# A Mamba, cross-attention and mixture-of-experts decoder layer on one core: the norm shift and seven FFN products move from VectorE to GpSimd, and all five orders are written anew

## The chip, the cores and the metric

One core of a Trainium2 chip runs the whole layer in one program. The metric is device time in microseconds (us) of that program; lower is better. The engines are called by their names in the profile: PE (TensorE), with its weight loads as PEld, DVE (VectorE), ACT (ScalarE), POOL (GpSimd) and SP (SyncE, which issues the DMAs here).

## What is computed

128 sequences of 64 tokens with 128 features, all in float32, go through three blocks. Each block adds its result to its input and normalises the sum over the features.

```python
x = layernorm(x + mamba(x))          # RMS norm, in-projection, 4-tap conv, silu, selective scan with 16 states, gate, out-projection
x = layernorm(x + xattn(x, ctx))     # 16 heads of width 8, over the 64 tokens of the same sequence's context
x = layernorm(x + moe(x))

def moe(xf):                         # 8 routed experts of width 176, top 2, and a shared one
    scores = softmax(xf @ w_router.T)
    topk_w, topk_idx = top_k(scores, 2)
    topk_w = topk_w / (topk_w.sum(-1) + 1e-20)
    cw = (one_hot(topk_idx, 8) * topk_w[..., None]).sum(1)
    eo = einsum(silu(xf @ wg) * (xf @ wu), wd)
    return einsum('te,teh->th', cw, eo) + silu(xf @ wg_s) * (xf @ wu_s) @ wd_s

def layernorm(x): return (x - mean(x)) / sqrt(var(x) + 1e-5)
```

## The kernel before

The tokens are cut into 16 chunks of 8 sequences, 512 tokens each. A full tile is 128 partitions by 512 columns. A chunk goes through these steps, under the names that the order lists use:

- `squares`, `mean`, `scaled`, `xnT`, `hid`, `gate`, `tap`, `taps`, `tanh`, `silu`, `gated_h`, `xp`, `less`, `dt`, `soft`, `soft_ln`, `delta`: the part of the Mamba block ahead of its scan.
- `decay`, `B_row`, `drive`, `scan`, `prod`, `y_sum`: the scan. For each of the 16 states and each of two halves of 128 channels ACT makes a decay tile, DVE a scan (L881), POOL the product with C (L1011) and PE adds that up in PSUM (L503). The scan tiles are 512 columns wide, before and after. For the four states in `JOINED`, POOL first adds two products (L1015), so PE has fewer sums.
- `gated`, `mout`, `stats`, `shift`, `norm`, `x1T`: out-projection and first LayerNorm. The three LayerNorms are numbered by halves: stats0 and stats1 the first, stats2 and stats3 the second, stats4 and stats5 the third.
- `k`, `v`, `q`, and `km` or POOL's `k`: the keys, eight times over with all but one head pair masked out (the tile `km`; POOL makes five of the eight masked copies, L1047 and L1050, ACT three). Then for each of 8 sequences `score` (PE), the row maximum (DVE, L932), `exp` (ACT, L767, eight pieces), `sum` (DVE, the reciprocal `rden`, L936), `scale` (POOL, L1056), `turn` (PE transposes, L575), `mix` (PE, L583), then `aout`.
- second LayerNorm, `x2T`, `route` (PE, L596), the router's arithmetic `route`, `r_rank`, `r_cw` on DVE and POOL, and `cwT`, which goes to DRAM (`cw_out`) and comes back spread over partitions (`cw_in`, slots `cwr`, two of them).
- the FFN: 13 tiles of 128 hidden features. PE makes `up_g` and `up_u` of a tile (L599), ACT the tanh of g (L806), DVE `(tanh + 1) * g` into `ga` (L979) and `ga * u` into `acts[i]` (L984), and POOL multiplies the first 11 tiles by the routing weights (`cw`, L1069). `down` (PE, L609 and L615) sums them up. The third LayerNorm and `out` end the chunk.

Two buffers tie the steps of neighbouring chunks together. `acts[0..7]` lie in the same memory as `km`, so the masked keys of a chunk can be written only after `down` of the chunk before it has read them, and that FFN's tiles only after the attention of its own chunk. `ga` lies in `kT`. The eight PSUM banks are two for `p_drive`, two for the sums `p_y` and a ring of four (`p_ring`) that all other PE results share, in the order in which PE makes them.

A norm's `stats` step makes mean and variance on DVE (L852, L856), POOL adds eps (L1028) and raises to the power -0.5 (L1031), DVE makes the shift `-mean * rstd` (L926), and ACT applies both (L791).

Each engine runs a fixed list of steps, once per turn: `ORDER_TEXT` gives it and it is written out in the file. A word such as `back.up_g3` means: step up_g3 of the chunk that is one turn behind the scan. `head`, `front`, `scan`, `back` and `tail` are chunks +2, +1, 0, -1 and -2 against the turn's own. So the list of a turn holds steps of up to five chunks side by side. An engine waits at a step until its inputs are there, and whatever stands behind it in the list waits too; the waits are semaphores.

## Time and profile before

| what | value |
|---|---|
| median of 3 runs | 2048.26 us (2046.75 to 2048.63) |
| the profiled execution's own time | 2052.23 us |
| its span, first to last instruction | 2050.4 us |
| mean granted PE clock | 0.934 of full speed |
| PE busy | 1716.5 us, 84% |
| DVE busy | 1687.0 us, 82% |
| ACT busy | 1362.9 us, 66% |
| POOL busy | 1418.6 us, 69% |
| DMA queue of SP | 23.9% of 16 engines |

No engine is full, and the lists are the same in each turn, so a middle turn can be read as one period. In a timeline each row has its start in us from the span's start, the duration of the group in us, the engine, the source line, the operation, the tiles written and read, and in brackets how long the engine sat idle before it and what ended the wait. Successive instructions overlap by some 0.1 us in the records, so the step from one start to the next is a little less than a duration.

### The profile page before, as it was taken

To read this page: it belongs to the slowest core of one execution; us is meant where nothing else is said; L and a number is where in the kernel's file an instruction comes from. 1 tells how busy PE (TensorE), PEld (TensorE's weight loads), DVE (VectorE), ACT (ScalarE), POOL (GpSimd) and SP (SyncE) were. 2 spreads that over 40 slices of the span, in tenths; PEclk is the share of its full clock that TensorE was granted. 3 is DMA by queue.
4 is the path that set the end of the run, shared out by engine and by line. 5 is a ranking of instruction groups with operands and counts; after the bars stand their busy time and mean duration, and the time that the engine had idled before them with its cause. 6 is when DMAs were issued, how large, how long until landed. Compare 5 with 4: busy or idle time off the path is not lost. (4 is left out here: it accounts for less than half of the span.)

```text
span 2050.4 us, 26488 instructions
## 1 busy us (share of the span) xinstructions
PE 1716.5 (84%) x7047; PEld 1002.7 (49%) x7138; DVE 1687.0 (82%) x2369; ACT 1362.9 (66%) x4258; POOL 1418.6 (69%) x1300
## 2 busy tenths in 40 slices
PE   3668897989889898988988898898989889897967
PEld 1224464545446454544645454464545546454544
DVE  3798888989888897988889898888988889887623
ACT  3569577685957768495775848677594866757361
POOL 0587677867767686777768687776867777686733
PEclk8779999999999999999999999999999999998988
DMA  3212322213232122323212232221222222122202
...
DMA packets 125926, 140.56 MB, mean 69 GB/s; under 512 B 44049, under 2 KB 69457, under 8 KB 125777
## 3 DMA queue, kind: packets, MB, share of 16 engines
q1 hardware_dynamic: 125776, 138.86, 23.9%
...
## 5 line engine op out<-in xcount | busy, mean ns | idle before, releaser
L1011 POOL TENSOR_TENSOR prod<-state,c_rep 128x512 f32<-128x512 f32 x512 | 668.5, 1313 | 87.6 <-DVE state L881 80.2
L881 DVE TENSOR_TENSOR_SCAN state<-decay,p_drive 128x512 f32<-128x512 f32 x512 | 610.4, 1206 | 25.0 <-ACT decay L637 17.3
L503 PE MATMUL p_y<-prod,ident 128*128 128x512 f32 x768 | 410.3, 621 | 6.0 <-POOL prod L1011 2.8
L637 ACT ACTIVATE decay<-delta,a_neg 128x504 f32<-128x504 f32 x512 | 364.7, 719 | 63.9 <-DVE state L881 60.5
L868 DVE TENSOR_TENSOR p_drive<-u,p_drive 128x1024 f32<-128x1024 f32 x256 | 312.3, 1220 | 69.6 <-PE p_drive L485 64.5
L767 ACT ACTIVATE ex<-p_ring,nmax 128x64 f32<-128x64 f32 x1024 | 305.5, 338 | 11.2 <-DVE nmax L932 9.5
L599 PE MATMUL p_ring<-x2T,wg 128*128 128x512 f32 x416 | 232.3, 643 | 6.5 <-DVE kT L979 6.5
L767 ACT ACTIVATION_READ_ACCUMULATOR ex<-p_ring,nmax 128x1 f32 x1024 | 237.4, 232 | 0.0
L1056 POOL TENSOR_TENSOR ex<-ex,rden 128x512 f32<-128x512 f32 x128 | 133.4, 1042 | 139.8 <-DVE rden L936 111.3
L806 ACT ACTIVATE gt<-p_ring 128x512 f32<-128x512 f32 x208 | 122.7, 590 | 160.1 <-PE p_ring L599 160.1
L599 PE MATMUL p_ring<-x2T,wu 128*128 128x512 f32 x416 | 217.4, 612 | 10.8 <-DVE kT L979 10.1
L503 PEld LDWEIGHTS p_y<-prod,ident 128*128 128x128 f32 x768 | 145.7, 199 | 142.4 <-issue 117.0
L1069 POOL TENSOR_TENSOR km<-km,cwr 128x512 f32<-128x512 f32 x128 | 162.6, 1271 | 26.9 <-DMA cwr<-cw_rows 26.6
L1015 POOL TENSOR_TENSOR prod<-prod 128x512 f32<-128x512 f32 x128 | 163.8, 1280 | 10.0
L583 PE MATMUL p_ring<-exT,vm 128*128 128x128 f32 x1024 | 143.4, 284 | 23.7 <-ACT exT L776 23.0
L583 PEld LDWEIGHTS p_ring<-exT,vm 128*128 128x128 f32 x1024 | 129.9, 194 | 65.8 <-issue 43.6
L979 DVE SCALAR_TENSOR_TENSOR kT<-gt,p_ring 128x512 f32<-128x512 f32 x208 | 140.4, 675 | 16.6 <-ACT gt L806 12.0
L570 PE MATMUL p_ring<-km,qs 128*128 128x512 f32 x256 | 132.0, 608 | 21.8 <-POOL km L1050 17.0
L575 PE MATMUL p_ring<-ident,ex 128*128 128x128 f32 x512 | 83.0, 287 | 78.9 <-POOL ex L1056 73.7
L599 PEld LDWEIGHTS p_ring<-x2T,wu 128*128 128x128 f32 x416 | 79.8, 198 | 115.0 <-issue 78.2
L615 PE MATMUL p_ring<-wd,km 128*128 128x128 f32 x1024 | 126.6, 277 | 4.7 <-POOL acts_more L1069 4.7
L791 ACT ACTIVATE x<-p_ring,shift,rstd 128x128 f32<-128x128 f32 x192 | 77.6, 461 | 73.9 <-DVE shift L926 73.9
...
## 6 DMA issues: line engine op xcount, KB each, us to landing
c_rep<-c_rows SPq DMA_DIRECT2D x256, 256.0 KB, 3.9
...
```

What stands on the lines that cost most here:

```text
L503: pe.matmul(p_y[1 - first][:], ident[:], prod[:, k % BUFFERS, :], start=False, stop=n == STATE - 1).then_inc(prod_used.sem, 1)
L583: mm = pe.matmul(p[:, 0:128], vm[:, i, q, :], exT[:, q, :], start=q == 0, stop=q == QUADS - 1)
L599: mm = pe.matmul(p[:], (wg if name == "up_g" else wu)[:, i, :], x2T[:], start=True, stop=True)
L637: act.activation(decay[:, j, :].rearrange("p (b t) -> p b t", t=SEQ)[:, :, 1:], delta[:, c.parity, j, :].rearrange("p (b t) -> p b t", t=S ...
L767: e = act.activation(ex[:, i % 2, a, :], p[:, a * SEQ:(a + 1) * SEQ], ACT.Exp, bias=nmax[:, i % 2, a:a + 1], accum_out=den[:, i % 2, a:a + 1])
L868: dve.tensor_tensor(p_drive[:], u[:, c.parity, :, :], p_b.unsqueeze(1).to_broadcast([128, HALVES, T]), ALU.mult).then_inc(drive_ready.sem, 1)
L881: dve.tensor_tensor_scan(state[:, k % BUFFERS, :], decay[:, j, :], p_drive[:, j, :], 0.0, ALU.mult, ALU.add).then_inc(state_ready.sem, 1)
L979: dve.scalar_tensor_tensor(ga, gt[:, i % 2, :], 1.0, p[:], ALU.add, ALU.mult).then_inc(free(name, i), 1)
L1011: pool.tensor_tensor(prod[:, k % BUFFERS, :], state[:, k % BUFFERS, :], c_rep[:, n % C_SLOTS, :], ALU.mult).then_inc(prod_ready.sem, 1)
L1015: pool.tensor_tensor(prod[:, k % BUFFERS, :], prod[:, k % BUFFERS, :], prod[:, (k - HALVES) % BUFFERS, :], ALU.add).then_inc(join_ready.se ...
L1056: pool.tensor_tensor(ex[:, i % 2, :, :], ex[:, i % 2, :, :], by_group(rden[:, i % 2, :]).to_broadcast([128, PAIRS, SEQ]), ALU.mult).then_i ...
L1069: pool.tensor_tensor(acts[i], acts[i], cwr[:, slot, :], ALU.mult).then_inc(act_ready.sem, 1)
```

## The change

`ON_POOL` names seven of the 13 FFN tiles. For these DVE writes `(tanh + 1) * g` straight into `acts[i]`, ACT copies u out of PSUM into one of two new tiles `us`, and a new POOL step `gu` multiplies the two; `cw` of that tile waits for it. The other six tiles are as before. ACT's copy of the third and later of the seven waits until POOL has used the same `us` tile, two tiles back.

The shift of all six norm halves is made by POOL: `nmean = -mean` beside the variance, then `shift = nmean * rstd` after `rstd`. DVE's `shift` step is gone.

The router's 1e-20 is a ninth column of `r_sel`, filled once, so that the sum over nine columns has it in, and the separate addition (L966) is gone. A reserve of memory for software DMAs is cut to 1024 bytes, which makes room for `us`; no DMA of this kernel is issued that way.

The order lists are new for all five engines, and are cut at another place of the period. Two lines of POOL's list stand for them in the diff.

```diff
--- before.py
+++ after.py
@@ -64,6 +64,7 @@
 ROUTED = EXPERTS * EXPERT_I // 128
+ON_POOL = (1, 2, 4, 5, 7, 8, 10)
 ROW_B, ROW_C = RANK, RANK + 3 * STATE
@@ -73,70 +74,68 @@
...
-        "scan.prod9 scan.prod10 scan.prod11 scan.prod12 back.scale3 scan.prod13 scan.prod14 "
...
+        "tail.cw10 back.stats0 back.stats1 scan.prod2 tail.stats4 scan.prod3 back.k0 tail.stats5 "
+        "scan.prod4 scan.prod5 back.scale0 scan.prod6 scan.prod7 back.scale1 scan.prod8 scan.prod9 "
@@ -256,7 +255,7 @@
         mhalf = sb("mhalf", [128, GROUPS])
-        eps = sb("eps", [128, 3])
+        eps = sb("eps", [128, 5])
 
@@ -288,6 +287,7 @@
         var = sb("var", [128, 3, GROUPS])
+        nmean = sb("nmean", [128, 3, GROUPS])
         rstd = sb("rstd", [128, 3, GROUPS])
@@ -313,7 +313,7 @@
         r_rank = sb("r_rank", [128, GROUPS, EXPERTS])
-        r_sel = sb("r_sel", [128, GROUPS, EXPERTS])
+        r_sel = sb("r_sel", [128, GROUPS, EXPERTS + 1])
         r_cw = sb("r_cw", [128, GROUPS, 128])
@@ -321,6 +321,7 @@
         r_gt, r_eq = pairwise[:, 0], pairwise[:, 1]
+        us = sb("us", [128, 2, T])
         acts_more = sb("acts_more", [128, FFN_TILES - CHUNK_B, T])
@@ -375,8 +376,9 @@
             signal(n, CHUNK_B) for n in ("max_ready", "rden_ready", "scale_ready"))
-        route_v, route_exp, route_g = signal("route_v", 11), signal("route_exp"), signal("route_g", 2)
+        route_v, route_exp, route_g = signal("route_v", 10), signal("route_exp"), signal("route_g", 2)
         gt_ready, act_ready = signal("gt_ready", FFN_TILES), signal("act_ready", ROUTED)
+        u_copied, gu_ready = signal("u_copied", len(ON_POOL)), signal("gu_ready", len(ON_POOL))
 
@@ -599,7 +601,7 @@
                 elif name == "cwT":
-                    pe.wait_ge(route_v.sem, route_v.at(c.m, 10))
+                    pe.wait_ge(route_v.sem, route_v.at(c.m, 9))
                     for g in range(GROUPS):
@@ -804,6 +806,14 @@
                     act.activation(gt[:, i % 2, :], p[:], ACT.Tanh, scale=0.5).then_inc(gt_ready.sem, 1)
+                elif name == "up_u":
+                    k = ON_POOL.index(i)
+                    p = filled(act, name, i, c.m)
+                    if k >= 2:
+                        act.wait_ge(gu_ready.sem, gu_ready.at(c.m, k - 2))
+                    elif c.m >= 1:
+                        act.wait_ge(gu_ready.sem, gu_ready.at(c.m - 1, len(ON_POOL) - 2 + k))
+                    act.activation(us[:, k % 2, :], p[:], ACT.Copy).then_inc(free(name, i), 1)
                 elif name == "cwT":
@@ -824,6 +834,8 @@
             dve.memset(eps[:, 1:3], LN_EPS)
+            dve.memset(eps[:, 3:5], -1.0)
+            dve.memset(r_sel[:, :, EXPERTS:], TOP_EPS)
             dve.memset(r_cw[:], 0.0).then_inc(consts_v.sem, 1)
@@ -919,12 +931,6 @@
                     ln_statistics(c, ln, half, filled(dve, LN_IN[ln], half, c.m))
-                elif name == "shift":
-                    ln, half = divmod(i, 2)
-                    g = slice(2 * half, 2 * half + 2)
-                    dve.wait_ge(ln_rstd[ln].sem, ln_rstd[ln].at(c.m, half))
-                    dve.scalar_tensor_tensor(shift[:, ln, g], mv[:, ln, g, 0], -1.0, rstd[:, ln, g],
-                                             ALU.mult, ALU.mult).then_inc(ln_shift[ln].sem, 1)
                 elif name == "score":
@@ -958,25 +964,28 @@
                     dve.wait_ge(route_v.sem, route_v.at(c.m, 5))
-                    dve.scalar_tensor_tensor(r_sel[:], r_rank[:], float(TOP), r_prob[:], ALU.is_lt, ALU.mult
+                    dve.scalar_tensor_tensor(r_sel[:, :, 0:EXPERTS], r_rank[:], float(TOP), r_prob[:], ALU.is_lt, ALU.mult
                                              ).then_inc(route_v.sem, 1)
...
                     dve.wait_ge(route_v.sem, route_v.at(c.m, 7))
-                    dve.tensor_scalar(r_max[:], r_sum[:], TOP_EPS, None, ALU.add).then_inc(route_v.sem, 1)
+                    dve.reciprocal(r_rec[:], r_sum[:]).then_inc(route_v.sem, 1)
                     dve.wait_ge(route_v.sem, route_v.at(c.m, 8))
-                    dve.reciprocal(r_rec[:], r_max[:]).then_inc(route_v.sem, 1)
-                    dve.wait_ge(route_v.sem, route_v.at(c.m, 9))
                     if c.m >= 1:
                         emptied(dve, "cwT", 0, c.m - 1)
-                    dve.tensor_tensor(r_cw[:, :, 0:EXPERTS], r_sel[:], by_group(r_rec[:]).to_broadcast(wide), ALU.mult
+                    dve.tensor_tensor(r_cw[:, :, 0:EXPERTS], r_sel[:, :, 0:EXPERTS], by_group(r_rec[:]).to_broadcast(wide), ALU.mult
                                       ).then_inc(route_v.sem, 1)
...
                     dve.wait_ge(gt_ready.sem, gt_ready.at(c.m, i))
-                    if i > 0:
-                        emptied(dve, "up_u", i - 1, c.m)
-                    dve.scalar_tensor_tensor(ga, gt[:, i % 2, :], 1.0, p[:], ALU.add, ALU.mult
+                    if i in ON_POOL:
+                        to = acts[i]
+                    else:
+                        to = ga
+                        last = max((j for j in range(i) if j not in ON_POOL), default=None)
+                        if last is not None:
+                            emptied(dve, "up_u", last, c.m)
+                    dve.scalar_tensor_tensor(to, gt[:, i % 2, :], 1.0, p[:], ALU.add, ALU.mult
                                              ).then_inc(free(name, i), 1)
@@ -1025,11 +1034,15 @@
                     pool.wait_ge(ln_aggr[ln].sem, ln_aggr[ln].at(c.m, half))
-                    pool.tensor_tensor(var[:, ln, g], mv[:, ln, g, 1], eps[:, 1:3], ALU.add
+                    pool.tensor_tensor(var[:, ln, g], mv[:, ln, g, 1], eps[:, 1:3], ALU.add)
+                    pool.tensor_tensor(nmean[:, ln, g], mv[:, ln, g, 0], eps[:, 3:5], ALU.mult
                                        ).then_inc(ln_var[ln].sem, 1)
...
                                        ).then_inc(ln_rstd[ln].sem, 1)
+                    pool.wait_ge(ln_rstd[ln].sem, ln_rstd[ln].at(c.m, half))
+                    pool.tensor_tensor(shift[:, ln, g], nmean[:, ln, g], rstd[:, ln, g], ALU.mult
+                                       ).then_inc(ln_shift[ln].sem, 1)
                 elif name == "add_out_b":
@@ -1062,8 +1075,16 @@
                     pool.tensor_tensor(r_gt, r_gt, r_eq, ALU.add).then_inc(route_g.sem, 1)
+                elif name == "gu":
+                    emptied(pool, "up_g", i, c.m)
+                    emptied(pool, "up_u", i, c.m)
+                    pool.tensor_tensor(acts[i], acts[i], us[:, ON_POOL.index(i) % 2, :], ALU.mult
+                                       ).then_inc(gu_ready.sem, 1)
                 elif name == "cw":
-                    emptied(pool, "up_u", i, c.m)
+                    if i in ON_POOL:
+                        pool.wait_ge(gu_ready.sem, gu_ready.at(c.m, ON_POOL.index(i)))
+                    else:
+                        emptied(pool, "up_u", i, c.m)
                     slot = i % CW_SLOTS
@@ -1146,7 +1167,7 @@
     arrays = {k: np.ascontiguousarray(v) for k, v in arrays.items()}
-    nc = bacc.Bacc("TRN2", target_bir_lowering=False, num_devices=1)
+    nc = bacc.Bacc("TRN2", target_bir_lowering=False, num_devices=1, dynamic_dma_scratch_size=1024)
     args = {k: nc.dram_tensor(f"in_{k}", v.shape, mybir.dt.from_np(v.dtype), kind="ExternalInput").ap()
...
```

How the instructions stand now is shown at three places. First, POOL between the router's ranking (L1061 and L1064 before, L1074 and L1077 now, tile x1T) and the first FFN tiles. Before:

```order
L1061 TENSOR_TENSOR x1T<-x1T,tri 128x256
L1064 TENSOR_TENSOR x1T<-x1T 128x256
L1011 TENSOR_TENSOR prod<-state,c_rep 128x512
L1015 TENSOR_TENSOR prod<-prod 128x512
L1011 TENSOR_TENSOR prod<-state,c_rep 128x512
L1015 TENSOR_TENSOR prod<-prod 128x512
L1011 TENSOR_TENSOR prod<-state,c_rep 128x512
L1023 TENSOR_TENSOR rms<-ms,mhalf 128x4
L1011 TENSOR_TENSOR prod<-state,c_rep 128x512
L1069 TENSOR_TENSOR km<-km,cwr 128x512 x2
```

and in the changed kernel, where L1081 is the new step `gu` and L1090 is `cw`:

```order
L1077 TENSOR_TENSOR x1T<-x1T 128x256
L1020 TENSOR_TENSOR prod<-state,c_rep 128x512
L1024 TENSOR_TENSOR prod<-prod 128x512
L1081 TENSOR_TENSOR km<-km,us 128x512
L1020 TENSOR_TENSOR prod<-state,c_rep 128x512
L1024 TENSOR_TENSOR prod<-prod 128x512
L1020 TENSOR_TENSOR prod<-state,c_rep 128x512
L1090 TENSOR_TENSOR km<-km,cwr 128x512
L1081 TENSOR_TENSOR km<-km,us 128x512
L1090 TENSOR_TENSOR km<-km,cwr 128x512
L1081 TENSOR_TENSOR km<-km,us 128x512
L1090 TENSOR_TENSOR km<-km,cwr 128x512
```

Products of the scan have moved out of this stretch, and the new multiplications stand in their place.

Second, POOL around the masked keys (km), between two of the scan's joins. Before:

```order
L1015 TENSOR_TENSOR prod<-prod 128x512
L1039 TENSOR_TENSOR x1b<-x,rowb 128x512
L1028 TENSOR_TENSOR var<-mv,eps 128x2
L1031 TENSOR_TENSOR rstd<-var,mhalf 128x2
L1047 TENSOR_TENSOR km<-kT,masks 128x8x64
L1050 TENSOR_SCALAR km<-kT,masks 128x8x64 x4
```

and in the changed kernel:

```order
L1024 TENSOR_TENSOR prod<-prod 128x512
L1060 TENSOR_TENSOR km<-kT,masks 128x8x64
L1063 TENSOR_SCALAR km<-kT,masks 128x8x64 x4
L1037 TENSOR_TENSOR var<-mv,eps 128x2
L1038 TENSOR_TENSOR nmean<-mv,eps 128x2
L1041 TENSOR_TENSOR rstd<-var,mhalf 128x2
L1044 TENSOR_TENSOR shift<-nmean,rstd 128x2
```

The last half of the third norm, which stood ahead of the keys, stands behind them, and the sum into x1b has moved to a later place.

Third, DVE at the first sequences of the attention: nmax is the row maximum, rden the reciprocal of the sum, h and gate are full tiles of the Mamba part. Before:

```order
L932 TENSOR_REDUCE nmax<-p_ring 128x8
L899 SCALAR_TENSOR_TENSOR h<-h,zc 128x512 x2
L903 SCALAR_TENSOR_TENSOR gate<-gate,gh 128x512
L932 TENSOR_REDUCE nmax<-p_ring 128x8
L936 RECIPROCAL rden<-den 128x8
L881 SCALAR_TENSOR_TENSOR state<-decay,p_drive 128x512
```

and in the changed kernel:

```order
L938 TENSOR_REDUCE nmax<-p_ring 128x8
L893 SCALAR_TENSOR_TENSOR state<-decay,p_drive 128x512
L938 TENSOR_REDUCE nmax<-p_ring 128x8
L942 RECIPROCAL rden<-den 128x8
L911 SCALAR_TENSOR_TENSOR h<-h,zc 128x512
L938 TENSOR_REDUCE nmax<-p_ring 128x8
```

Ahead of the first rden there now stand a scan and the second row maximum, where the two h tiles, a gate tile and the second row maximum stood.

## Rows read from the trace of the kernel before

**Rows 1.** The page's head line.

```profile
span 2050.4 us, 26488 instructions
```

**Rows 2.** One DVE line of the router, once per chunk: duration, start in us.

```profile
L956 DVE TENSOR_TENSOR x1T<-r_prob x1: 418/418/418, 215.8 to 215.8; 128x256 f32<-128x256 f32 x1
...
L956 DVE TENSOR_TENSOR x1T<-r_prob x1: 419/419/419, 1780.0 to 1780.0; 128x256 f32<-128x256 f32 x1
```

**Rows 3.** Busy us (x instructions) of PE, PEld, DVE, ACT, POOL; clock, DMA.

```profile
1055.45:1099.03 43.58, 42.21 (x115) 19.29 (x117) 38.56 (x56) 22.39 (x48) 33.60 (x28) 0.94 0.37 110
1099.03:1113.76 14.73, 14.68 (x122) 13.84 (x122) 12.75 (x27) 6.53 (x14) 10.94 (x14) 1.00 0.01 2
1113.76:1119.21 5.45, 4.09 (x21) 2.56 (x21) 5.42 (x7) 5.39 (x15) 5.45 (x7) 1.00 0.00 0
1119.21:1166.82 47.61, 39.50 (x172) 23.00 (x175) 40.85 (x51) 43.07 (x183) 36.74 (x32) 1.00 0.29 78
1166.82:1174.96 8.14, 3.77 (x17) 2.62 (x16) 6.62 (x9) 7.24 (x11) 2.46 (x4) 0.71 0.00 0
sum 119.51, PE 104.25 PEld 61.31 DVE 104.19 ACT 84.62 POOL 89.20; mean PE 20.85 PEld 12.26 DVE 20.84 ACT 16.92 POOL 17.84
```

**Rows 4.** Timeline around down's end and the masked keys.

```profile
1111.75 0.38 PE L551 MATMUL p_ring<-ident,x 128*128 128x128 f32 x2
...
1111.97 1.02 PE L494 MATMUL p_y<-h,diag_d 128*128 128x512 f32 x2
...
1113.76 1.04 POOL L1047 TENSOR_TENSOR km<-kT,masks 128x512 f32<-128x512 f32 x1
```

**Rows 5.** Timeline at the attention's first sequence.

```profile
1120.95 2.80 DVE L899 SCALAR_TENSOR_TENSOR h<-h,zc 128x512 f32<-128x512 f32 x2
...
1123.19 0.34 ACT L767 ACTIVATE ex<-p_ring,nmax 128x64 f32<-128x64 f32 x1
...
1123.68 1.75 DVE L903 SCALAR_TENSOR_TENSOR gate<-gate,gh 128x512 f32<-128x512 f32 x1
...
1125.95 0.19 DVE L936 RECIPROCAL rden<-den 128x8 f32<-128x8 f32 x1
...
1127.47 0.63 PE L575 MATMUL p_ring<-ident,ex 128*128 128x128 f32 x4 [3.51 <-POOL ex L1056]
```

**Rows 6.** Timeline from the second norm's last half to the FFN.

```profile
1167.88 0.20 POOL L1028 TENSOR_TENSOR var<-mv,eps 128x2 f32<-128x2 f32 x1 [0.74 <-DVE mv L856]
1168.16 0.71 POOL L1031 TENSOR_TENSOR rstd<-var,mhalf 128x2 f32<-128x2 f32 x1
...
1168.90 1.22 DVE L926 SCALAR_TENSOR_TENSOR shift<-mv,rstd 128x2 f32<-128x2 f32 x1
...
1171.10 0.79 ACT L791 ACTIVATE x<-p_ring,shift,rstd 128x128 f32<-128x128 f32 x2
...
1173.26 1.85 PE L596 MATMUL p_ring<-wrt,x2T 128*128 128x8 f32 x8 [0.56 <-ACT x2T L796]
```

**Rows 7.** First and last routing product of the period on POOL.

```profile
1072.05 1.27 POOL L1069 TENSOR_TENSOR km<-km,cwr 128x512 f32<-128x512 f32 x1 [0.46 <-DMA cwr<-cw_rows]
...
1099.56 1.26 POOL L1069 TENSOR_TENSOR acts_more<-acts_more,cwr 128x512 f32<-128x512 f32 x1
```

**Rows 8.** Groups by line and shape: busy us, mean ns | idle before, releasers.

```profile
L881 DVE TENSOR_TENSOR_SCAN state<-decay,p_drive 128x512 f32<-128x512 f32 x512 | 610.4, 1206 | 25.0 <-ACT decay L637 17.3 <-POOL prod L1011 0.7
...
L984 DVE TENSOR_TENSOR km<-kT,p_ring 128x512 f32<-128x512 f32 x128 | 87.9, 686 | 36.6 <-PE p_ring L599 27.9 <-DVE kT L979 0.5
...
L776 ACT ACTIVATE exT<-p_ring 128x512 f32<-128x512 f32 x128 | 77.5, 606 | 15.8 <-PE p_ring L575 12.9 <-PE p_ring L583 0.6
...
L966 DVE TENSOR_SCALAR r_max<-r_sum 128x4 f32<-128x4 f32 x16 | 15.4, 965 | 0.6
```

**Rows 9.** Lines of their own: ns min/median/max, first and last start.

```profile
L926 DVE SCALAR_TENSOR_TENSOR shift<-mv,rstd x96: 146/994/1236, 147.2 to 2046.1; 128x2 f32<-128x2 f32 x96
...
L899 DVE SCALAR_TENSOR_TENSOR h<-h,zc x32: 666/1200/1754, 32.7 to 1724.1; 128x512 f32<-128x512 f32 x32
```

115 rows, old and new, of the table ORDER_TEXT are left out of this document.

## The prediction, made before the changed kernel ran

> **What bounds the kernel now.** I read the head line first [rows 1], then one router line that runs once per chunk: from its first start to that of chunk 13 there are 13 equal periods in 1564.2 us, 120.3 us each [rows 2]. The kernel is these periods, with 215.8 us ahead and 270 us behind in which fewer stages run. The view by stretches of one such period (119.5 us) shows what kind of bound it is [rows 3]: in the sum PE is busy 104.3 us, DVE 104.2, POOL 89.2, ACT 84.6. No engine is the limit over the period; each is the limit somewhere. What closes into a ring is one chunk's way through the shared memory of `km` and `acts`: masked keys, attention, second norm, router, FFN, down, and then the next chunk's keys. Its length is the period, so I price the change along that ring, in the five stretches of [rows 3]: FFN up to the start of down 43.6 us, down to the start of the keys 14.7, keys 5.5, attention 47.6, and from its end to the first FFN product 8.1. What each is short of can be read there: the FFN stretch has PE at 42.2 and DVE at 38.6 of 43.6; attention has ACT at 43.1 of 47.6; the last has everything waiting, and the PE clock falls to 0.71.
>
> **Work moved, per chunk.** DVE loses seven products of 0.69 us (4.8) [rows 8], six shifts (median 0.99, least 0.15, so 4 to 6, [rows 9]) and one addition of 0.97 [rows 8]: about 10 of 104 us. ACT gains seven copies out of PSUM, by the nearest row (a 128x512 copy, 0.61) 4.3 us [rows 8]: 88.9. POOL gains seven products of 1.27 [rows 7] and twelve two-column operations, by the variance row 0.20 each [rows 6], 11.3 in all: 100.5 of 119.5. POOL goes from third to first or second.
>
> **Down to the keys.** POOL starts the masked keys at 1113.76, though down's last product was through by 1111.75 when PE took the next step; between them stands the third norm's half [rows 4]. In the new list that half stands behind the keys: 1.9 us less, if the join ahead of them ends in time. Two pairs of x1T transposes now stand between the halves of down, 0.22 us each by the distance of the starts in [rows 4]: 0.45 more. Sum -1.45; from -1.9 to -0.5 if POOL is late by one product. Keys to first score: 0, PE waits for them now as before.
>
> **Attention.** In its first sequence the last exp piece ends at 1123.5, but its reciprocal is at 1125.95, because two h tiles and a gate tile stand ahead of it on DVE; the first transposes wait for POOL's scale until 1127.47, 3.51 us of idle PE [rows 5]. The new DVE list has the reciprocal right behind the second row maximum: 2.4 us less. On ACT one pair of dt copies leaves the stretch, 1.2 us by [rows 8], and ACT is what is full here. Against that POOL gets 4.2 us more work between keys and last scale: two bias additions (2.5), one norm half (1.3) and 0.4 for the other. POOL idles 10.9 us in the stretch now [rows 3], and every scale has to come in time. So the bounds are -3.6 (POOL's new work fits its gaps) and +0.6 (all of it is on the path). I find no row that settles it and take the middle, -1.5.
>
> **Second norm to FFN.** Now: POOL's rstd ends at 1168.87, DVE's shift takes 1.22 to 1170.12, but ACT norms only at 1171.10, being in the softplus table switch; route starts at 1173.26 and at the low clock takes 1.85 [rows 6]. So removing the handoff to DVE alone would give nothing here: ACT is late next. In the new list the softplus steps stand behind the first FFN tiles. From the end of aout (1166.82): variance 1.1 later as now, then 0.28, 0.28, 0.7 and 0.25 to the shift, 2.6. ACT has gate1 and a decay ahead of the norm; gate1 waits for two PE products of 0.9 [rows 4], then 0.6 each: 3.0. The norm 0.8, the dt pair that now stands behind it 1.2, x2T 0.4, route at full clock half of 1.85: first FFN product at 6.4 instead of 8.14. -1.7, from -2.5 (ACT in time) to +0.5 (dt late as well). PE has gate, two sums and two dt products there, where it now idles 4.4 of the 8.1 us [rows 3], so the clock should stay up.
>
> **FFN.** The router's chain loses the addition, 0.97, and DVE's wait for the first up_u product (27.9 us in 16 chunks, 1.74 each, [rows 8]), since that product no longer runs behind others at the low clock; a scan of 1.2 [rows 8] now stands inside the chain, half hidden by the exp: -2.1 up to the first `cw`. From there to down POOL works through 11 `cw`, six `gu`, five products of the scan and rms: 22 x 1.27 + 1.0 - 1.27 (down needs only the tenth) = 27.7 us, where it was 1099.03 - 1072.05 = 27.0 with waits for the cwr DMAs in it [rows 3, 7]: +0.7. PE has 38 us of work in the stretch against 42 and DVE some 35 (their lists counted by the same durations), so both have cover. The gated and delta steps move in here. A DVE instruction with two SBUF inputs is stretched when POOL runs beside it: h takes 0.67 alone and 1.75 at worst [rows 9]. For delta and u I take +1.0, with 0 and +2.2 as bounds, on POOL as well. Sum -0.4, from -2.8 to +2.9.
>
> The Trainium skill states the rule behind that row (SBUF — State Buffer, "Who interferes with whom"): an instruction of VectorE with two SBUF inputs and one of GpSimd that reads SBUF take the same read interface, and the second is fully blocked until the first has ended. The two-column shift agrees, 0.15 us at best and 1.24 at most for the same work [rows 9]. By that rule the change cuts both ways: seven operations fewer on DVE to be blocked, and more GpSimd time in which taps, silu, gated, delta and u are.
>
> **Sum.** -1.45 - 1.5 - 1.7 - 0.4 = -5.05 us per period. I count it 14 times, 13 periods and one for both ends, where fewer stages overlap: -71 us. The profiled execution took 2052.23 us (span 2050.4), 4.0 above the median of the runs, so 1981.5 there and **1978 us** as a median.
>
> **Rivals.** (1) Small gain: the stretches in which ACT was late shrink (second norm, -1.7) and the keys start early, but POOL's scales and `gu` come late by what attention and router had gained. -1.45 - 1.7 + 0.6 + 0.4 = -2.1, x14: 2018 us. For it: POOL would be at 100.5 of 117. Against: the first sequence's wait is plain. (2) Slower, POOL as the bound: POOL idles 119.5 - 89.2 = 30.3 us a period because it waits for others by its list [rows 3]. If 25 of these stay, the period is 125.5 and the time 2048 + 14 x 6 = 2132 us; it decides at 19 us of idle. Its place: a `us` copy on ACT waits for `gu` two tiles back, that stands behind `cw` waiting for a DMA, and behind the copy wait tanh, decays and with them the scans. Against: POOL's longest idle now (in the 8.1 us stretch it works 2.5) is where the path itself shrinks. (3) Large gain: attention at its lower bound and more, as ACT, POOL and DVE all lose their first wait; the limit is POOL's 100.5 at 90% use, 111.7: -7.8 x 14, 1939 us. (4) The gains don't add up, since the scan's own chain (drive, two scans) fills in: no change, 2048.
>
> **Chances.** Forecast 0.50 (its own range 1945 to 2005), small gain 0.22, large gain 0.12, no change 0.04, slower 0.12. A measurement of this kernel can tell about 0.2%, 4 us. Faster 0.84, same 0.04, slower 0.12. The range that leaves out 2 in 10 runs from 1930 to 2035: slower and no change lie outside, and the end of the large gain.
>
> **What would show it.** The router line's distance, 115 us instead of 120. Masked keys starting within 0.3 us of down's last product. The idle ahead of the first transposes in a chunk under 1.5 us instead of 3.5. No stretch with a clock of 0.7 ahead of the FFN. POOL at 100 us per period. DVE about 94. I am wrong if POOL's waits for `us`, `rden` or the cwr DMAs grow to more than they were, or if ACT sits behind a `us` copy for more than 2 us a tile.

## The result, and the profile after

The changed kernel takes **1972.6 us** (median of 4 runs, 1966.4 to 1976.8) against 2047.6 for the kernel before beside it: ratio 0.9627, 95% interval 0.9605 to 0.9650. The forecast was 1978 us. The total is right, but by luck: two of its terms were off by 4 us a period, in opposite directions.

The head of the page, and the router line again, which runs once per chunk (ns min/median/max, first and last start), beside [rows 1, 2]:

```profile
span 1975.0 us, 26883 instructions
...
PE 1691.8 (86%) x7138; PEld 975.5 (49%) x7138; DVE 1544.2 (78%) x2147; ACT 1407.3 (71%) x4370; POOL 1584.2 (80%) x1604
```

```profile
L962 DVE TENSOR_TENSOR x1T<-r_prob x16: 415/418/420, 207.4 to 1918.2; 128x256 f32<-128x256 f32 x16
```

The profiled execution lost 75.4 us of span (2050.4 to 1975.0). The five stretches of one period, the view of [rows 3]:

```profile
1010.15:1058.18 48.03, 42.19 (x121) 19.68 (x121) 40.38 (x56) 30.73 (x63) 40.60 (x35) 0.93 0.28 90
1058.18:1071.65 13.47, 13.47 (x122) 13.43 (x121) 12.72 (x19) 5.94 (x14) 9.73 (x16) 1.00 0.00 0
1071.65:1076.41 4.76, 3.54 (x15) 1.67 (x13) 1.82 (x5) 4.72 (x11) 4.68 (x8) 1.00 0.00 0
1076.41:1119.65 43.24, 38.62 (x174) 22.89 (x175) 36.91 (x48) 41.07 (x179) 37.97 (x37) 1.00 0.31 86
1119.65:1126.21 6.56, 6.43 (x24) 2.69 (x22) 4.30 (x8) 4.62 (x10) 6.25 (x9) 1.00 0.24 80
1010.15:1126.21 116.06, 104.26 (x449) 60.37 (x448) 96.13 (x133) 87.08 (x274) 99.22 (x101) 0.97 0.24 74
```

One period is a sample. I took the same marks (first up product, first down product, masked keys on POOL, first score, end of aout, next up product) from the timelines of twelve steady periods of every kernel. Mean us; the kernels below the second line are the experiments, told further down:

| kernel | FFN | down to keys | keys | attention | norm to FFN | period |
|---|---|---|---|---|---|---|
| before | 43.26 | 14.73 | 5.45 | 48.76 | 8.14 | 120.33 |
| changed | 47.00 | 13.46 | 4.76 | 43.28 | 6.54 | 115.05 |
| *change, forecast* | *-0.4* | *-1.45* | *0* | *-1.5* | *-1.7* | *-5.05* |
| *change, measured* | *+3.74* | *-1.27* | *-0.69* | *-5.48* | *-1.60* | *-5.28* |
| a: old lists, no products on POOL | 42.59 | 15.51 | 4.83 | 48.47 | 8.07 | 119.48 |
| b: new lists, no products on POOL | 51.44 | 13.47 | 4.76 | 43.26 | 6.54 | 119.47 |
| c: copy of u1 first | 44.73 | 13.47 | 4.76 | 43.38 | 6.56 | 112.89 |
| d: silu back | 45.57 | 13.47 | 4.76 | 43.71 | 6.53 | 114.03 |
| e: gate tile back | 43.51 | 13.59 | 4.75 | 44.25 | 6.55 | 112.65 |
| f: softplus back | 48.80 | 13.47 | 4.76 | 43.40 | 15.86 | 126.29 |
| g: old lists, products on POOL | 50.43 | 15.94 | 4.84 | 48.46 | 8.09 | 127.76 |
| h: c and d | 44.13 | 13.49 | 4.76 | 43.48 | 6.55 | 112.41 |
| j: silu, gate and dt back | 45.53 | 13.48 | 4.76 | 45.46 | 6.49 | 115.72 |
| k: c, e and the copy of u10 | 41.32 | 15.29 | 4.76 | 44.68 | 6.55 | 112.61 |
| l: k and gu2 first | 43.49 | 13.47 | 4.76 | 44.43 | 6.55 | 112.70 |
| m: j and product 3 back | 44.92 | 13.47 | 4.76 | 49.36 | 6.36 | 118.87 |

Attention won 4.0 us more than forecast and the FFN stretch lost 4.1 more, so the sum hit by luck. The steps that the forecast had followed instruction by instruction came out as told. Down's last product is followed by PE's next step at 1071.34 and the keys start 0.31 us later, where 2.0 us lay between [rows 4]; the second norm now runs on POOL in one row (timeline: start, duration):

```profile
1071.65 1.04 POOL L1060 TENSOR_TENSOR km<-kT,masks 128x512 f32<-128x512 f32 x1 [1.49 <-PE p_ring L617]
...
1121.33 0.19 POOL L1037 TENSOR_TENSOR var<-mv,eps 128x2 f32<-128x2 f32 x1
1121.48 0.20 POOL L1038 TENSOR_TENSOR nmean<-mv,eps 128x2 f32<-128x2 f32 x1
1121.75 0.71 POOL L1041 TENSOR_TENSOR rstd<-var,mhalf 128x2 f32<-128x2 f32 x1
1122.54 0.20 POOL L1044 TENSOR_TENSOR shift<-nmean,rstd 128x2 f32<-128x2 f32 x1
```

ACT norms at 1122.77, 0.03 after the shift, where it came 0.98 after it [rows 6], and the clock in that stretch is 1.00 instead of 0.71.

The surprise stands in the FFN stretch. ACT, POOL and PE at its start, in the same period (ahead of each bracket: idle time, and who ended it):

```profile
1018.35 0.60 ACT L808 ACTIVATE gt<-p_ring 128x512 f32<-128x512 f32 x1 [2.11 <-PE p_ring L601]
1018.85 0.59 ACT L816 ACTIVATE us<-p_ring 128x512 f32<-128x512 f32 x1
```

```profile
1019.58 1.27 POOL L1081 TENSOR_TENSOR km<-km,us 128x512 f32<-128x512 f32 x1 [2.19 <-ACT us L816]
1020.81 1.26 POOL L1020 TENSOR_TENSOR prod<-state,c_rep 128x512 f32<-128x512 f32 x1
```

```profile
1023.47 1.59 PE L505 MATMUL p_y<-prod,ident 128*128 128x512 f32 x2 [2.85 <-POOL prod L1024]
1024.86 0.63 PE L487 MATMUL p_drive<-xp,sel_bc 128*128 128x512 bf16 x1
1025.28 2.94 PE L601 MATMUL p_ring<-x2T,wg 128*128 128x512 f32 x4
```

The copy of u1 had its data at 1016.4 (PE made it from 1014.50 on), but it stands behind the tanh of tile 2, whose product is ready 2 us later. POOL's first new multiplication waits for the copy, the scan's join waits behind it, PE waits 2.85 us for the join, and the four matmuls behind it take 2.94 us, where four take 1.88 at full clock. Over the whole run POOL waits for the copies, and PE for the join (us, times, longest):

```profile
POOL km L1081 <- ACT us L816: 36.9, 28, 5.4
```

```profile
PE p_y L505 <- POOL prod L1024: 41.2, 18, 2.9
```

The FFN stretch can be split into the time that PE is busy in it and the time that it waits. The same work is busy for longer where the granted clock is low. Mean of the twelve periods, us:

| kernel | FFN | PE busy | PE waits | granted clock |
|---|---|---|---|---|
| before | 43.26 | 41.35 | 1.9 | 0.95 |
| changed | 47.00 | 41.09 | 5.9 | 0.95 |
| b | 51.44 | 40.83 | 10.6 | 0.98 |
| c | 44.73 | 38.99 | 5.7 | 1.00 |
| d | 45.57 | 39.55 | 6.0 | 0.98 |
| e | 43.51 | 38.36 | 5.2 | 0.99 |
| k | 41.32 | 37.72 | 3.6 | 1.00 |

So what the changed kernel loses here against the kernel before is PE's waits.

### The profile page after: what moved, and what is told of

It reads as the page before. It is cut to its first block and busy times, and to the rows that moved or that the text cites. A ratio compares the mean times of both kernels' runs of the same rounds, so it can differ in the third digit from the quotient of the medians.

```text
span 1975.0 us, 26883 instructions
## 1 busy us (share of the span) xinstructions
PE 1691.8 (86%) x7138; PEld 975.5 (49%) x7138; DVE 1544.2 (78%) x2147; ACT 1407.3 (71%) x4370; POOL 1584.2 (80%) x1604
## 5 line engine op out<-in xcount | busy, mean ns | idle before, releaser
L1020 POOL TENSOR_TENSOR prod<-state,c_rep 128x512 f32<-128x512 f32 x512 | 647.0, 1277 | 39.4 <-DVE state L893 20.8
L505 PE MATMUL p_y<-prod,ident 128*128 128x512 f32 x768 | 414.5, 630 | 41.2 <-POOL prod L1024 41.2
L769 ACT ACTIVATION_READ_ACCUMULATOR ex<-p_ring,nmax 128x1 f32 x1024 | 255.7, 254 | 0.0
L505 PEld LDWEIGHTS p_y<-prod,ident 128*128 128x128 f32 x768 | 139.7, 198 | 173.8 <-issue 97.8
L601 PE MATMUL p_ring<-x2T,wu 128*128 128x512 f32 x416 | 201.8, 599 | 11.5 <-DVE km L988 11.5
L1069 POOL TENSOR_TENSOR ex<-ex,rden 128x512 f32<-128x512 f32 x128 | 137.5, 1075 | 74.6 <-DVE rden L942 44.9
L1090 POOL TENSOR_TENSOR km<-km,cwr 128x512 f32<-128x512 f32 x128 | 168.5, 1321 | 20.6 <-DMA cwr<-cw_rows 20.5
L1024 POOL TENSOR_TENSOR prod<-prod 128x512 f32<-128x512 f32 x128 | 172.2, 1346 | 10.0
L601 PEld LDWEIGHTS p_ring<-x2T,wg 128*128 128x128 f32 x416 | 82.8, 214 | 128.3 <-issue 68.4
L1081 POOL TENSOR_TENSOR km<-km,us 128x512 f32<-128x512 f32 x80 | 112.9, 1412 | 36.9 <-ACT us L816 36.9
```

The lines of the kernel that those rows point to most:

```text
L505: pe.matmul(p_y[1 - first][:], ident[:], prod[:, k % BUFFERS, :], start=False, stop=n == STATE - 1).then_inc(prod_used.sem, 1)
L601: mm = pe.matmul(p[:], (wg if name == "up_g" else wu)[:, i, :], x2T[:], start=True, stop=True)
L769: e = act.activation(ex[:, i % 2, a, :], p[:, a * SEQ:(a + 1) * SEQ], ACT.Exp, bias=nmax[:, i % 2, a:a + 1], accum_out=den[:, i % 2, a:a + 1])
L1020: pool.tensor_tensor(prod[:, k % BUFFERS, :], state[:, k % BUFFERS, :], c_rep[:, n % C_SLOTS, :], ALU.mult).then_inc(prod_ready.sem, 1)
L1024: pool.tensor_tensor(prod[:, k % BUFFERS, :], prod[:, k % BUFFERS, :], prod[:, (k - HALVES) % BUFFERS, :], ALU.add).then_inc(join_ready.se ...
L1069: pool.tensor_tensor(ex[:, i % 2, :, :], ex[:, i % 2, :, :], by_group(rden[:, i % 2, :]).to_broadcast([128, PAIRS, SEQ]), ALU.mult).then_i ...
```

## The experiments

Each ratio is to the kernel before on the same chip, with its 95% interval. The edits are to the lists of the changed kernel unless said otherwise.

**a and b: the small edits without the new lists, and the new lists without the products.** a has the old lists with shift on POOL and the eps column:

```
-ON_POOL = (1, 2, 4, 5, 7, 8, 10)
+ON_POOL = ()
```

> The kernel before with its own order lists; only the six shifts move to POOL and the router's addition becomes a ninth column. No product moves. Theory 1 (the gain comes from the new lists, which the moved products make room for): DVE is full in the FFN stretch (38.6 of 43.6 us) and loses there 1 us of the router chain, while the shift on DVE at the second norm was covered by a late ACT; so 0.5 to 1.5 us a period, 2025 to 2040 us. Rival (the two-column shifts, blocked for up to 1.2 us behind POOL's products, are themselves what costs): 5 us a period come back from DVE, 1975 to 1995 us. Third: the ending of a norm now stands on POOL behind a product, no gain, 2048.

Measured 2037.1 us, ratio 0.9940 (0.9922 to 0.9958), within theory 1's range: 0.85 us per period, -0.67 of it in the FFN stretch, where the addition left the router. The stretch from attention to FFN is unchanged, 8.07: taking the handoff to DVE away gives nothing while ACT is late, as the forecast had it.

b has the new lists and the small edits, with every product of u on DVE behind its gate product and no copies.

> The changed kernel with its new lists, but all 13 products with u stay on DVE (each right behind its g step; no copies on ACT, no gu on POOL). Per chunk DVE gets 4.8 us back, ACT loses 4.1 and POOL 8.9. Theory 1 (the FFN stretch, 4.4 us longer in the changed kernel, is long because POOL and the copies hold it up): this is as fast as the changed kernel or faster, 1940 to 1975 us. Rival (the moved products are what pays, DVE would be full again in the FFN): 1985 to 2030 us.

Measured 2044.9, ratio 0.9983 (0.9957 to 1.001). My theory fell, and the rival's range (1985 to 2030) was too mild: the new order, with the small edits, gives nothing in sum. It gives all of the 5.5 us in attention, and pays 8.2 in the FFN stretch. DVE is the fullest there, 45.4 of one stretch's 51.4 us (columns as in [rows 3]), PE waits 6.1 us of the stretch for DVE's gate products in the mean, and the seven products on POOL are worth 4.4 us:

```profile
1160.10:1211.47 51.37, 40.12 (x121) 18.14 (x121) 45.44 (x63) 27.83 (x56) 32.05 (x28) 1.00 0.28 83
```

**g: the old lists with the products on POOL.** Copies and products put in by hand:

```
 ACT   back.up_g1 +back.up_u1 back.cwT0 +back.up_u2 ... back.up_g5 +back.up_u4 back.up_g6 ...
 POOL  head.mean0 scan.prod25 +back.gu1 back.cw0 +back.gu2 back.cw1 ... +back.gu4 back.cw2 ...
```

> The lists of the kernel before, with the shift and the eps column as in the changed kernel, and the seven products on GpSimd added to them by hand: each copy of u on ScalarE behind the tanh of the next tile, each product on GpSimd one step ahead of the cw multiplication before its own. Together with the run that had the same lists and no products (2037 us) it tells what the products give alone. Theory A (the products pay in any lists, because VectorE is what is full in the FFN stretch: 38.6 of 43.6 us there): FFN stretch 2 to 4 us shorter per period, attention unchanged at 48.5, 1985 to 2015 us. Rival B (only lists made for them have room for the copies and for 6 more GpSimd products in that stretch): FFN stretch the same or longer, 2035 to 2080 us.

Measured 2158.9, ratio 1.0525 (1.0507 to 1.0542). The rival was right and too mild. This is the slower case of the prediction (2132 us there) by its main reason: POOL's work in the FFN stretch grows from 33.3 us in a to 41.0, and its idle time by the list stays (9.3 us in a, 9.4 here), so the stretch grows with the work. The place that the prediction named plays a small part. The first product stands behind the root of the next chunk's norm, which waits for ACT, and not behind a `cw` that waits for a DMA. The third copy does wait for a us buffer, but ACT's waits of this kind are 8.8 us in the whole run.

```profile
1248.93 1.02 POOL L1034 TENSOR_TENSOR rms<-ms,mhalf 128x4 f32<-128x4 f32 x1 [4.38 <-ACT ms L660]
1249.92 1.26 POOL L1022 TENSOR_TENSOR prod<-state,c_rep 128x512 f32<-128x512 f32 x1
1251.14 1.27 POOL L1083 TENSOR_TENSOR km<-km,us 128x512 f32<-128x512 f32 x1
```

```profile
1252.51 0.60 ACT L818 ACTIVATE us<-p_ring 128x512 f32<-128x512 f32 x1 [0.91 <-POOL km L1083]
```

So no part does it alone (small edits -0.6%, lists with the small edits -0.2%, which the interval doesn't tell from nothing, products with the small edits +5.3%); all of them together give -3.7%.

**c: the copy of u1 first.** To test the chain read above:

```
 ACT   back.up_g1 front.soft0 +back.up_u1 back.up_g2 -back.up_u1 back.cwT0
```

> The changed kernel with one pair swapped in ACT's list: the copy of u1 stands ahead of the tanh of tile 2 instead of behind it. In the trace the copy waits for that tanh's matmul, POOL's first product waits 2.2 or 0.5 us for the copy, POOL's join stands behind that product, and PE waits 2.9 or 1.9 us for the join, after which its clock falls in some periods. Theory (that chain is on the path): 1 to 3 us a period less than the changed kernel, 1930 to 1958 us. Rival (the routing products' DMA chain is the pace, PE's wait is slack): no change, 1968 to 1977 us.

Measured 1942.4 us, ratio 0.9467 (0.9450 to 0.9484), 1.7% less than the changed kernel's. The FFN stretch is 2.3 us shorter, nothing else moves. POOL's first new product follows without a wait, and the join ends 8.0 us after the start of POOL's router step, where it took 10.2 above:

```profile
1008.19 1.26 POOL L1027 TENSOR_TENSOR prod<-prod 128x512 f32<-128x512 f32 x1
1009.41 1.27 POOL L1084 TENSOR_TENSOR km<-km,us 128x512 f32<-128x512 f32 x1
1010.71 1.27 POOL L1023 TENSOR_TENSOR prod<-state,c_rep 128x512 f32<-128x512 f32 x1
1012.06 1.26 POOL L1027 TENSOR_TENSOR prod<-prod 128x512 f32<-128x512 f32 x1
```

The chain is on the path, but most of what it costs is paid through the clock. PE's wait for the join falls by 1.0 us in the mean, but its waits for DVE grow by 0.9, so all its waits in the stretch fall by only 0.2. Its busy time falls by 2.1 with the same instructions. In the three periods in which the changed kernel keeps its full clock, its FFN stretch is 45.1 to 45.3 us, close to c's 44.7.

**d: the silu products back ahead of the first reciprocal.** This is the 2.4 us of the forecast's term for attention:

```
 DVE   back.score1 +front.silu0 +front.silu1 back.sum0 -front.silu0 back.score2 ... -front.silu1
```

> The changed kernel with both h tiles (silu) put back ahead of the first reciprocal of the attention on DVE, as they stood before. They take 0.67 us each alone, up to 1.75 beside POOL. Theory (the first head's wait is most of what the attention gave, 4.4 us a period): 0.7 to 2.5 us a period more, 1984 to 2012 us. Rival (attention is paced by ACT being full and the first head has slack): under 0.3 us a period, 1970 to 1978 us.

Measured 1956.4, ratio 0.9546 (0.9528 to 0.9565). Refuted: attention is 0.4 us longer, not 2.4, and the whole is 0.8% faster, by a shorter FFN stretch. PE waits as long in that stretch as without the edit, 6.0 us; it is busy 1.5 us less, at a mean clock of 0.98 instead of 0.95, which is the whole gain of 1.4. With c in place the same edit (h) adds nothing that can be told, which fits: both mainly keep the clock up. How the silu products' place does that, the trace doesn't name.

**e: the first gate tile back in attention.**

```
 PE    back.score0 +front.gate0     (from ahead of back.v0)
 ACT   back.exp0 +front.gate0       (from ahead of scan.k0)
 DVE   back.score0 +scan.gated_h0   (from behind back.up_u6 of the FFN)
```

> The changed kernel with one thing put back into attention: the first gate tile (its TensorE product behind score 0, its ScalarE copy behind the first exp, the VectorE product gated_h0 behind the first row maximum), where the kernel before has them. Attention is 5.5 us per period shorter in the changed kernel, against 1.5 forecast. Theory A (attention is short because work left it, each of the three engines being nearly full there): attention grows by 1.5 to 2.5 us per period, the FFN stretch shrinks by 0.5 to 1, in all +1 to +2 per period, 1985 to 2000 us. Rival B (what counts is where the scan steps and reciprocals stand, a gate tile more finds room): attention +0 to +0.6, the whole 1965 to 1980 us.

Measured 1944.8, ratio 0.9474 (0.9454 to 0.9494). Both theories had the whole slower or about equal; it is 1.6% faster than the changed kernel. Attention pays 1.0, the FFN stretch gets 3.5 us shorter. Of these 3.5 us, 0.9 is the gate product that left PE, 0.8 less waiting, and 1.8 less time at the low clock.

**h: c and d together.**

> The changed kernel with both edits that made it faster: the copy of u1 ahead of the tanh of tile 2 on ScalarE, and both silu products ahead of the first reciprocal on VectorE. Theory A (they remove different waits): the gains of 2.2 and 1.0 us per period add up, about 111.9 us per period and 1923 to 1933 us. Rival B (both only keep TensorE's clock from falling at the start of the FFN stretch, which the first edit does alone): 1939 to 1950 us, as with the first edit alone, or slower by the 0.4 us that attention loses.

Measured 1940.2, ratio 0.9460 (0.9446 to 0.9474), no different from c: rival B.

**f: softplus back ahead of the second norm.**

```
 ACT   back.x2T0 front.gate1 +front.dt0 +front.dt1 +front.soft0 +front.soft_ln0 scan.decay26 back.norm3
 PE    front.dt0 +front.dt1 scan.B_row13 back.x2T1 -front.dt1
```

> The changed kernel with the four softplus steps of ScalarE (two Relu/Abs pairs, Exp, Ln) ahead of the second norm's second half, as in the kernel before, and the second dt product ahead of the x2 transposes on TensorE. Theory A (the term of the prediction: ScalarE sits between the shift and the norm): the stretch from attention's end to the first FFN product grows from 6.5 us by 2 to 4.5 us, of which the FFN stretch gives back at most 2, since ScalarE is rid of the steps there: +1 to +3 per period, 1985 to 2015 us. Rival B (the steps cost the FFN stretch as much as they cost here, since they stand ahead of the copy of u1 there): the sum within 0.7 us per period of the changed kernel, 1963 to 1983 us.

Measured 2135.3, ratio 1.0415 (1.0399 to 1.0431), outside both ranges: the stretch is 9.3 us longer. ACT is at it from 1221.15 to 1228.54 and PE waits 7.62 us, after which route and FFN start at half clock (0.51 from 1231.3 to 1238):

```profile
1223.82 1.06 ACT L724 ACTIVATE sp_a<-sp_a 128x1024 f32<-128x1024 f32 x1
1224.90 1.28 ACT L728 ACT_TABLE_LOAD   x1
1226.19 1.06 ACT L728 ACTIVATE sp_a<-sp_a 128x1024 f32<-128x1024 f32 x1
1227.26 1.28 ACT L642 ACT_TABLE_LOAD   x1
```

```profile
1230.11 0.66 PE L556 MATMUL p_ring<-ident,x 128*128 128x128 f32 x2 [7.62 <-ACT x L796]
1231.34 1.85 PE L601 MATMUL p_ring<-wrt,x2T 128*128 128x8 f32 x8 [0.56 <-ACT x2T L801]
1233.04 2.05 PE L604 MATMUL p_ring<-x2T,wg 128*128 128x512 f32 x2
```

In the old lists the same steps lay ahead of a later shift and cost 1 us there [rows 6]. Here gate1 and its wait stand ahead of them, so this run shows the price of the place in the new lists and is no clean undoing of the old term. The Trainium skill (ScalarE: Activation LUTs, "What ACT_TABLE_LOAD costs") gives a switch of tables 1.28 us for the load and 1.38 more of drain, 2.66 in all. The load agrees. The drain isn't here: the load starts 0.02 us after the end of the instruction ahead of it, and the next one 0.01 us after the load's end.

**j and m: what had left attention, put back together.** j is e with d's edit in the old order, and the dt pair:

```
 DVE   back.score0 +front.silu0 +front.silu1 +scan.gated_h0 scan.scan8 back.score1
 ACT   back.exp6 +front.dt0
```

> The changed kernel with all that had left attention put back together: both silu products and gated_h0 ahead of the first reciprocal on VectorE, in the old order, the first gate tile on TensorE and ScalarE, and the first dt pair behind the fifth exp. One at a time, the silu products had lengthened attention by 0.4 us and the gate tile by 1.0. Theory A (ScalarE is what sets attention; before, it stood 1.9 us per period waiting to write the gate tile until VectorE had taken the old one, behind the silu products): 43.3 + 1.9 (that wait) + 0.6 (the gate copy) + 1.2 (the dt pair) = 47.0, so 46.3 to 48.0 us of the 48.8 before. Rival B (moves find room of their own, and attention is short for another reason, such as the order of GpSimd's scales): 0.4 + 1.0 + at most 1.2 more, 44.5 to 45.9 us. The FFN stretch stays near the 43.5 us that it had with the gate tile alone moved; in all 1985 to 2010 us by A, 1950 to 1975 by B.

Measured 1985.0, ratio 0.9683 (0.9666 to 0.9700). For attention this is rival B: 45.5, that is 2.2 of the 5.5 us. The total isn't (1950 to 1975 by B; 1985.0 is the lower end of A), because the FFN stretch came out at 45.5 and not near 43.5, with a mean clock of 0.95. The dt pair stands behind `exp6` here, and not behind the fifth exp, as the expectation has it. m also moves POOL's product 3 with its join behind the keys:

```
 POOL  tail.stats4 -scan.prod3 back.k0 +scan.prod3 tail.stats5 scan.prod4 scan.prod5 back.scale0
```

> The kernel of the run before that had put back into attention all that had left it (45.5 us of attention per period, where the changed kernel has 43.3 and the kernel before 48.8), and one more step in its old place: GpSimd's product 3 with its join (2.5 us) behind the masked keys instead of ahead of them, so that four GpSimd products run beside the two silu products and gated_h0 as in the kernel before. There GpSimd stood idle 3.7 us ahead of the first scale in the trace looked at, so 2.5 us of work have room. Theory A (what was slow in the kernel before is this meeting: VectorE's three products with two SBUF inputs took 4.4 us there and 2.9 without the GpSimd products, and the first scale comes late by both): attention 47.3 to 49.0 us, the first silu pair and gate near 4.4 us again, TensorE's idle time ahead of the first transposes over 2 us, in all 2010 to 2040 us. Rival B (the products find room in that idle time): attention 45.0 to 46.2 us, 1975 to 2000 us in all, and what makes attention of the kernel before 3 us longer stays open.

Measured 2030.0, ratio 0.9912 (0.9880 to 0.9944), attention 49.4. The total is theory A's and attention lies 0.4 above its range, but the rows aren't A's: PE's wait for POOL's scales, which A wanted over 2 us at the first transposes, is under 0.1 us per period. The meeting of POOL and DVE products is worth 1.1 us (the silu pair 3.29, in j 2.20). More comes from a chain through the third norm: DVE's scan waits 7.61 us for a state buffer that product 3 gives back, the statistics stand behind that scan, then POOL's shift, ACT's norm, and PE's gate product; the clock falls behind it (four score products 3.15 us, in j 1.88).

```profile
1219.32 1.22 DVE L896 TENSOR_TENSOR_SCAN state<-decay,p_drive 128x512 f32<-128x512 f32 x1 [7.61 <-POOL prod L1023]
...
1222.84 3.29 DVE L914 SCALAR_TENSOR_TENSOR h<-h,zc 128x512 f32<-128x512 f32 x2
```

```profile
1222.73 0.81 ACT L796 ACTIVATE x<-p_ring,shift,rstd 128x128 f32<-128x128 f32 x2 [1.44 <-POOL shift L1047]
```

```profile
1223.59 2.08 PE L534 MATMUL p_ring<-xnT,win 128*128 128x512 f32 x2 [3.48 <-ACT x L796]
...
1227.16 3.15 PE L575 MATMUL p_ring<-km,qs 128*128 128x512 f32 x4
```

With these steps in their old places the gain is all but gone (118.9 of 120.3 us). But the kernel before has its statistics ahead of that scan, so m shows how much one POOL step's place can cost, not what it did cost there.

**k and l: a better version.** k has e, c, and the copy of u10 ahead of the first xn transpose, since PE waited 1.44 us per period for it:

```
 ACT   back.up_g11 +back.up_u10 head.xnT0 front.decay2 -back.up_u10 head.xnT1
```

> An attempt at a better version: the changed kernel with the first gate tile back in attention (2.4 us per period less, alone), the copy of u1 ahead of the tanh of tile 2 (2.2 less, alone), and the copy of u10 ahead of the first xn transpose on ScalarE, since TensorE waits 1.4 us per period for it at the second one. Theory A (each removes a wait of TensorE, which has 5 us of them in the FFN stretch): 112.6 - 1.0 to 2.5 = 110.2 to 111.6 us per period, 1900 to 1925 us. Rival B (gate tile and u1 copy were two cures of the same low clock at the start of the FFN stretch, and GpSimd's 40 us there are the next limit): 1930 to 1948 us.

> The same with GpSimd's product for tile 2 ahead of the first cw multiplication, which waits 1 to 2 us per period for the transfer of its row. Theory A (GpSimd is near its limit in the FFN stretch, 40 of 44 us): 0.5 to 1.5 us per period less than the same without it, 7 to 20 us. Rival B (that idle time is not on the path, TensorE's own 42 us are): within 3 us of it.

k measured **1932.4 us**, ratio 0.9427 (0.9405 to 0.9449), the lowest median here, 2.1% under the changed kernel's ratio, and in rival B's range; its interval overlaps h's. The gains of c and e don't add up: the FFN stretch falls to 41.3, and down to keys grows to 15.3, since PE has now caught up with POOL's last cw multiplications (it waits 0.9 us per period for them within down). l measured 1941.8, ratio 0.9471 (0.9457 to 0.9485). POOL's wait for the transfer falls from 1.7 to 0.5 us a period in the FFN stretch, and PE's wait for DVE's gate products there rises from 0.9 to 2.3. Its steady periods are those of k, 112.7 and 112.6, as rival B has it, but the whole is 9.4 us slower, which neither range has. The two profiled executions differ by 3.9 us, 1.2 of them in the twelve steady periods; where the rest of the 9.4 lies stays open. c, e, h, k and l all stop at 112.4 to 112.9 us per period. That is about what the changed kernel's own periods take when they keep the full clock (112.8 to 113.5). What holds them there stays open.

## Why the prediction came out right, and where it was wrong

The total hit by luck. The two terms of 4 us that were off are the subject of the paragraphs on attention and FFN.

**What bounds it, and the counts: right.** The ring of stretches held, and the ends' 14th period too (5.28 x 14 = 74 of 75.4 us). POOL's work in a period is 99.2 us (forecast 100.5), ACT's 87.1 (88.9), DVE's 96.1 (94).

**Down to keys, norm to FFN: right** in mechanism and size, -1.27 and -1.60. **Keys: small miss**, -0.7: the masked copies take 696 ns on average where they took 994, with DVE busy for 1.8 us of the stretch instead of 5.4, and now PE waits for ACT's q instead.

**Attention: the step that failed.** The forecast read one idle time of 3.51 us [rows 5], named the h tiles ahead of the reciprocal, and set its gain at 2.4. The wait did go:

```profile
1082.67 0.63 PE L577 MATMUL p_ring<-ident,ex 128*128 128x128 f32 x4 [0.71 <-POOL ex L1069]
```

Over all transposes of the stretch PE's wait for POOL's scales fell from 4.8 us a period to 1.5. But d puts the h tiles back and costs 0.4, and j has both h tiles and the gate tile ahead of the reciprocal again with PE's wait for the scales at 0.5. So the h tiles' place wasn't where the time lay. The forecast also put what leaves ACT at 1.2 us. ACT is nearly full in this stretch: in the mean over twelve it went from 43.3 of 48.8 us to 41.1 of 43.3, and in j, with the work put back, it is at 43.2 of 45.5. So 2.2 us of the gain are work that left the stretch, and the other 3.3 are idle time of ACT that j doesn't bring back (5.5 us before, 2.2 in the changed kernel, 2.3 in j). The largest part of it is one wait: ACT's copy of the gate tile waited 1.9 us a period for DVE's gate product, and in j, in the same place, it waits 0.2. POOL's waits for DVE shrank too; in the kernel before, over the whole run (us, times, longest):

```profile
POOL ex L1056 <- DVE rden L936: 111.3, 77, 5.2
...
POOL prod L1011 <- DVE state L881: 80.2, 58, 9.3
```

and in the changed one 44.9 and 20.8:

```profile
POOL ex L1069 <- DVE rden L942: 44.9, 29, 4.1
...
POOL prod L1020 <- DVE state L893: 20.8, 14, 2.8
```

I read this as the scan running further ahead of the attention's row maxima, so that POOL, PE and ACT wait for DVE less all along the stretch and not only at its first sequence. That reading isn't shown, and which of the moved steps does it wasn't isolated. The lower bound of the term, -3.6, assumed a single wait and was too tight.

**FFN: the other step that failed**, -0.4 against +3.7, outside the term's own range of -2.8 to +2.9. Up to the first cw the chain won 1.4 us in the period shown (15.2, before 16.6) and 1.2 in the mean, of the forecast's 2.1. The addition is gone, but DVE's wait for the first up_u product, which was to vanish with the low clock, does so only where the clock stays up: it is 0.1 us in five of the twelve periods and 1.8 in the other seven. The forecast had also priced it too high, at 1.74: its row has 32 waits in 16 chunks, and the first product's own was 1.4 in the mean of the twelve. For delta and u the forecast took +1.0; their means went from 1278 and 1285 ns to 1641 and 1884, together +0.96.

What failed is "both have cover", said of PE and DVE. The count behind it was good: PE was put at 38 us of work, and in the periods with a full clock it is busy 38.9. But new waits of PE were put at nothing, and they grew from 1.9 to 5.9 us a period, which is the whole loss. The largest are 2.4 for the join, 1.4 for a copy of u and 1.4 for DVE's gate products. And the clock, which was to stay up, is 1.00 ahead of the FFN but falls within it in nine of the twelve periods, so PE's busy time is 41.1 us in the mean, 2.2 more than the same work takes at full clock. The forecast had put POOL on the path with 27.7 us from the first cw to down. In the period shown it takes 32.9 us against 27.0; POOL's last cw ends at 1055.6, and down starts at 1058.18, held by PE's own queue. c and e take 2.3 and 3.5 us of it back, 2.1 and 1.8 of that as time at the low clock.

**The slower rival** named the copies waiting for products two tiles back. In the changed kernel that is 4.8 us in the whole run; the wait that hurt is the other way round, POOL's for a copy in line behind a tanh (36.9 us).

## What to carry to other kernels

A sum that fits proves nothing about its terms: read the stretches one by one after the run, since two misses of 4 us hid each other here. When work is handed from a full engine to two others, look at the first instruction of the new chain in each queue and ask what stands ahead of it: one copy moved by one place gave 1.7%, over two fifths of what the whole change had. And a count of an engine's work gives its cover only if its waits and its clock stay as they were: here the count of PE's work was right within 1 us, and the stretch still grew by 3.7, by PE's waits. When an edit in such a stretch gives more than the wait it removes, look at the granted clock and at the busy time of the same instructions.

## What the runs showed of the chip

The changed kernel's twelve steady periods have the same instructions and come in three kinds: three take 112.8 to 113.5 us, two 114.5 to 114.7, and seven 115.8 to 116.3. PE's busy time in the FFN stretch is 38.9, 40.5 and 42.2 us in them. The difference is the granted clock, which is 1.00 throughout in the first kind, falls to half for a while behind the wait for the join in the second, and in the third does so both at the FFN's start and behind that wait. Each fall costs 1.7 us of busy time; the one at the start also makes the join later, so that PE waits 2.9 us for it and not 1.9.

In the first window below, ahead of the FFN, a period of the third and one of the first kind both have a full clock and PE busy 6.4 and 6.5 of 7 us. Then one falls in part of the next window, with PE busy all the while (first of each pair: a 116 us period, second: one of 113; the last pair starts 9.9 and 9.0 us into the FFN):

```profile
1002.00:1009.00 7.00, 6.37 (x21) 2.77 (x21) 5.67 (x9) 4.96 (x12) 6.69 (x9) 1.00 0.22 75
1234.00:1241.00 7.00, 6.52 (x21) 2.77 (x21) 5.64 (x9) 5.00 (x12) 6.69 (x9) 1.00 0.24 77
...
1009.00:1016.00 7.00, 6.87 (x19) 3.40 (x19) 3.89 (x11) 3.90 (x8) 5.33 (x6) 0.76 0.01 4
1241.00:1248.00 7.00, 6.88 (x23) 3.56 (x23) 5.50 (x14) 4.01 (x7) 5.28 (x7) 1.00 0.00 0
...
1020.00:1027.00 7.00, 4.15 (x8) 1.47 (x7) 6.07 (x6) 5.08 (x6) 6.24 (x6) 0.79 0.34 115
1251.00:1258.00 7.00, 5.14 (x13) 1.92 (x11) 6.29 (x6) 6.89 (x10) 5.72 (x6) 1.00 0.34 116
```

So the two falls together cost a period about 3 us, and no row tells why the clock falls in the one kind and not in the other. In c, whose waits for the join are 1.4 us, it falls once in twelve periods, at the FFN's start, and all but two of the periods lie between 112.1 and 113.1 us.

For delta and u the least time is 1.22 us, which is also their median in the kernel before. In the changed kernel, with POOL busy beside them, the median is 1.87 and 2.17. POOL's shift takes 0.20 at the median and 0.54 at most, where DVE's took 0.99 and 1.24 for the same two columns [rows 9]. In the period shown POOL's own products beside delta and u took 1.52 and 2.25 us, at 1025.33 and 1026.81, where they take 1.27 otherwise.

The Trainium skill that the prediction drew on (SBUF — State Buffer, "Who interferes with whom") has it that a VectorE instruction with two SBUF inputs contends with a GpSimd instruction that reads SBUF. The rows of delta, u and POOL's products agree, and they show both engines paying.
